# The reads of the preceding group ahead of the products of the group, in a vision tower with linear attention on one core

## The reference

```python
h = _L0_tok_ref(x, gamma, beta, W, b)                       # (64, 169, 128)
h = concatenate([cls_tok, h], axis=1)
# attention over layernorm(h): q, k, v = x Wq^T, x Wk^T, x Wv^T
def step(S, qkv):
    qt, kt, vt = qkv
    S = S + LR * einsum('bd,be->de', vt, kt)                # summed over the 64 images
    return S, einsum('de,be->bd', S, qt)
h = h + outs
h = h + ffn(layernorm(h))
```

## Time and profile before

| | us |
|---|---|
| median of 3 runs | 224.33 |
| lowest, highest | 224.09, 224.41 |
| span of the profiled execution | 221.7 |
| TensorE multiply busy | 198.4 (89%) |
| TensorE weight load busy | 168.0 (76%) |
| VectorE busy | 152.6 (69%) |
| GpSimd busy | 152.1 (69%) |
| ScalarE busy | 128.6 (58%) |

### The profile page before, as it was taken

How to read it: one execution, slowest core, us unless ns; L and a number is a source line. 1 busy time by engine, 2 the same in 40 slices (tenths; PEclk the granted TensorE clock), 3 DMA queues, 4 the chain that set the end, 5 groups by cost and what they waited for, 6 DMA issues and landing times.

```text
span 221.7 us, 5075 instructions
## 1 busy us (share of the span) xinstructions
PE 198.4 (89%) x1566; PEld 168.0 (76%) x1566; DVE 152.6 (69%) x760; ACT 128.6 (58%) x314; POOL 152.1 (69%) x125
## 2 busy tenths in 40 slices
PE   0699998999899999999999999999999999988700
PEld 0499897787688889888888888889888888876500
DVE  4549894453397694678687587669579578779681
ACT  4232637797533464475756575574665566467972
POOL 1029938796972899969999859949999253262641
PEclk9999999999999999999999999999999999999975
DMA  5999991924022004253052422012202202202156
GB/s 137 398 419 423 416 418 69 269 98 162 10 74 90 6 0 166 50 159 97 3 178 76 162 50 49 19 33 50 47 3 49 47 3 49 47 4 47 31 116 148
DMA packets 17074, 25.90 MB, mean 117 GB/s; under 512 B 1576, under 2 KB 13551, under 8 KB 16920
## 3 DMA queue, kind: packets, MB, share of 16 engines
q1 hardware_dynamic: 16300, 25.06, 35.0%
q10 hardware_dynamic: 748, 0.51, 0.8%
HBM read 19.65 MB, written 5.92 MB: 115 GB/s over the span
## 4 chain that ended last, share of the span: by engine, by line
PE 69%; DMA 9%; DVE 7%; ACT 5%; SPq 3%; issue 3%; POOL 1%; POOLq 1%; ACTq 0%; DVEq 0%
PE conv L542 31%; PE vr_ps L586 12%; PE outs L613 9%; DMA images<-x_rows 9%; PE first_ps L596 8%; PE turn L576 4%; DVE dve L1191 2%; PE conv L550 2%; ACT values L780 1%; ACT scaled L750 1%; PE conv L586 1%; SPq L461 1%; DVE state L951 1%; ACT g_t L744 1%; DVE state L943 1%
## 5 line engine op out<-in xcount | busy, mean ns | idle before, releaser
L542 PE MATMUL conv<-scaled,wt 128*128 128x256 f32 (+3 forms) x432 | 111.3, 373 | 7.4 <-DMA wt<-weight 7.2
L444 POOL TENSOR_TENSOR scaled<-rows,gam 128x832 f32<-128x832 f32 (+1 forms) x54 | 83.9, 1573 | 17.7 <-DMA rows<-x_windows 17.5
L542 PEld LDWEIGHTS conv<-scaled,wt 128*128 128x128 f32 x432 | 71.8, 193 | 15.8 <-DMA wt<-weight 7.2
L780 ACT ACTIVATE values<-vr_ps,rstd 128x256 f32<-128x256 f32 x76 | 36.0, 474 | 61.4 <-PE vr_ps L586 52.2
L1266 POOL TENSOR_TENSOR rstd<-var,powers 128x8 f32<-128x8 f32 (+2 forms) x20 | 30.3, 1516 | 27.2 <-DVE var L963 27.1
L943 DVE TENSOR_TENSOR state<-first_ps,state 128x128 f32<-128x128 f32 x80 | 23.3, 291 | 31.2 <-PE first_ps L596 26.4
L788 ACT ACTIVATE images<-images,ln_shift,ln_gain 128x128 f32<-128x128 f32 x82 | 38.0, 488 | 1.6 <-DVE ln_shift L1014 1.6
L1256 POOL TENSOR_TENSOR g_low<-g_t,g_high 128x512 fp32r<-128x512 f32 x21 | 26.7, 1271 | 8.2 <-ACT g_high L767 8.2
L586 PE MATMUL vr_ps<-w_high,g_low 128*128 128x256 f32 x78 | 31.1, 398 | 0.3 <-ACT values L780 0.3
L932 DVE BATCH_NORM_STATS2 ln_stats<-images 128x6 f32<-128x128 f32 x85 | 23.8, 285 | 6.7 <-ACT images L774 6.6
L951 DVE TENSOR_TENSOR state<-second_ps,state 128x128 f32<-128x128 f32 x80 | 22.6, 282 | 2.1
(11 more groups left out here) (175 smaller groups left out, 267.1 us busy)
## 6 DMA issues: line engine op xcount, KB each, us to landing
rows<-x_windows SPq DMA_DIRECT2D x12, 864.0 KB, 5.0
out<-images SPq DMA_DIRECT2D x40, 128.0 KB, 2.4
images<-x_rows SPq DMA_DIRECT2D x4, 832.0 KB, 14.7
images<-x_rows SPq DMA_DIRECT2D x1, 1040.0 KB, 14.2
images<-x_rows SPq DMA_DIRECT2D x1, 624.0 KB, 20.5
rows<-x_windows SPq DMA_DIRECT2D x1, 448.0 KB, 6.3
gam<-gamma SPq DMA_DIRECT2D x1, 422.5 KB, 7.0
bet<-beta SPq DMA_DIRECT2D x1, 422.5 KB, 7.5
```

Source lines behind the costliest of these rows:

```text
L444: return eng.tensor_tensor(scaled[:, s, at + skip:at + N], window[:, skip:N], gains.unsqueeze(2).to_broadcast([P, N - skip, B]), ALU.mult)
L542: last = pe.matmul(conv_ps[g % 2][:, at:at + n * B], held, scaled[:, s, a % RING:a % RING + n], start=first, stop=(g < EARLY and s >= TOP ...
L780: act.activation(values[:, t % VALUE_SLOTS].rearrange("p a e -> p (a e)"), vr_bank(t)[:, 0:2 * E], ACT.Identity, scale=rho_of(t)).then_inc ...
```

## The change

In the first step of a period the call of the reads of group g - 1, with its wait for h2_ready, now stands ahead of the products of group g. The wait for the states of the preceding group stays first. It holds for g = 1 to 17; g = 0 has no reads, and the tail is as it was. The unused name WARM goes, so that all line numbers behind it are lower by one.

```diff
--- before.py
+++ after.py
@@ -31,7 +31,6 @@
 
 EARLY = 5
 
-WARM = 14
 LEAD = 2
@@ -632,10 +631,10 @@
                 if i == 0 and g >= 0:
                     if g > 0:
                         pe.wait_ge(state_ready, states_to(t - 1))
-                    products(g)
                     if g > 0:
                         pe.wait_ge(h2_ready, tile_no(t - PER_GROUP - 1))
                         reads(g - 1)
+                    products(g)
```

## The result

| | kernel before | changed kernel |
|---|---|---|
| median of 9 runs, us | 224.09 | 225.47 |
| span of the profiled execution, us | 221.7 | 223.4 |

The ratio of changed to before is 1.0079 with a 95% interval of 1.0051 to 1.0107: 0.8% slower, some 1.8 us by the ratio, 1.4 us by the medians and 1.6 us by the two spans before rounding (the last store is issued at 218.16 us in the kernel before and at 219.76 us in the changed one). The forecast was 1.49 us more and 225.8 us. In several kernels a few runs lie 1.7 to 2.7 us above the median; the ratios count them as well, and their intervals are the wider for it.

The account below looks back on a forecast made before the run. The prediction took TensorE to bound the kernel, with 198.4 us of work in a 221.7 us span. To the median of 224.33 us it added 0.46 and 1.03 us, giving 225.8 us, range 224.5 to 227.0.

Parts of the forecast that it names:

- TensorE's own time: Swapped blocks on TensorE keep their lengths behind new neighbours: 0 us, bounded at about 0.1 us in a period.
- What comes earlier: Reads end 1.09 us sooner, but add_out on VectorE stands behind later state sums, so nothing gains: 0 us.
- The first loss: At g = 1, VectorE's sum of group 4 ends later, so TensorE's turn of that group loses 0.46 us.
- The second loss: GpSimd's gapless string from g = 2 delays the power for group 6 and TensorE's vr product at g = 5: 1.03 us.
- The 0.32 us of waiting: TensorE's vr product at 94.93 us already waits 0.32 us in the kernel before, so that place has no room.
- Where it just fits: Other places, such as reads waiting for add_out, later vr products, scales and the tail, have just enough room: 0 us.
- the fit that was told as 0.00: After GpSimd's next long string, TensorE's vr product at 127.15 us is possible exactly when due: room 0.00, no loss.
- The sum: Whole kernel: 0.46 and 1.03 us added, span 223.2 us, median 225.8 us, 0.66% slower.
- B: GpSimd's string starts from something else or TensorE catches up: 0.46 us or less, 224.3 to 224.8 us; chance 0.11.
- C: TensorE's new block joins hide exposed weight loads: 0.1 us gained per period and join, down to 223.4 us; chance 0.06.
- D: Tight fits tip over or a TensorE join costs 0.1 us more: 226.1 to 227.0 us; chance 0.13.
- E: The new TensorE stop at 95 us, about 1.3 us long, drops its clock to 1.2 GHz: near 229 us; chance 0.02.

Follow-up runs that it names:

- only1: Kernel before with reads moved ahead of products at g = 1 alone; +0.46 us between two fixed TensorE rows, ratio 1.0043 to the kernel before.
- only2: Kernel before with reads moved ahead of products at g = 2 alone; +1.01 us between two fixed TensorE rows, ratio 1.0028 to the kernel before.
- after_pool: Changed kernel with four GpSimd scales moved behind the powers for groups 5 and 6; +0.20 us between two fixed TensorE rows, ratio 1.0009 to kernel before.
- not12: Kernel before with reads moved ahead of products only at g = 3 to 17; 0.00 us between two fixed TensorE rows, ratio 1.0006 to kernel before.
- after_both: Changed kernel with whole(g) ahead of VectorE's moments and four GpSimd scales behind the powers; median 223.06 us, ratio 0.9944 to the kernel before.
- before_both: Kernel before with whole(g) ahead of VectorE's moments and four GpSimd scales behind the powers; median 223.01 us, ratio 0.9947 to the kernel before.

## Why the prediction was right

**TensorE's own time, 0.** Right: 1.03 and 1.09 us in the new order, and 0.02 us between the two orders when both places have room. The bound of 0.1 us in a period was far wider than needed.

**What comes earlier, 0.** Right: the reads of group 5 start at 102.31, add_out of its group on VectorE follows its state sums as before, and net of the start-up no instruction of VectorE, ScalarE or GpSimd behind the turn of group 0 starts earlier than before by more than 0.02 us.

**The first loss, 0.46 us.** Right: 0.46 us in only1 and between the rows at 66 us.

**The second loss, 1.03 us more.** Right in its sum and its place, with 1.01 us in only2. The 0.32 us of waiting that it read at this place before were there, but were worth 0.26 us (after_pool). The prediction told one step less than there is: the loss comes in two parts. The first vr behind the power for group 5 loses 0.3 us (below, 0.81 us behind the convolution where before it was 0.52), and the one behind the power for group 6 the rest. Both hang on the same string, and what the first takes the second no longer has to.

```profile
86.68 0.82 PE L541 MATMUL conv<-scaled,wt 128*128 128x128 f32 x4
87.49 0.36 PE L585 MATMUL vr_ps<-w_high,g_low 128*128 128x256 f32 x1
```

**Where it just fits, 0.** Right on the whole. The vr product behind the fit that was told as 0.00 starts here:

```profile
128.73 0.47 PE L585 MATMUL vr_ps<-w_high,g_low 128*128 128x256 f32 x1
```

That is 1.58 us behind the 127.15 of the earlier trace rows, and the vr product before it, 125.19 against 123.62, was 1.57 us late already: the fit held. From 96.48 to the tail the delay grows from 1.55 to 1.60 us in steps of 0.01 or 0.02 us, too small to name a cause.

**The sum.** 1.49 us forecast, 1.53 us by the ruler, 1.6 us by the spans, of which 0.07 us is the start-up. The 225.8 us lie 0.3 us above the median of the runs, mainly because the median of before was 224.33 us in the three runs that the forecast started from, and 224.09 in nine.

**The rivals.** B (no change) fell with only1 and only2, C and D (the joins) with the block lengths and not12, and E with the first row of the clock below: TensorE is busy 1.75 of 2.5 us around the new stop, and the granted clock stays at its full level, 2.4 GHz. The row that the prediction leaned on had only 0.66 us without work, half of the stop of 1.3 us that it foresaw, so it couldn't speak against E by itself. Measured, the new stop is 1.45 - 0.35 = 1.10 us from start to start, 0.75 us of it idle. The rule of the Trainium skill that the prediction weighed here ("TensorE: Matmul & The Clock Gate", section "What's actually happening": idleness lowers the clock) isn't contradicted by it: this stop did not set it off, but with no TensorE work at all from 216 to 220 us the granted clock is at its lower level, 1.2 GHz (the second row).

```profile
94.50:97.00 2.50, 1.75 (x18) 1.26 (x15) 0.48 (x4) 1.14 (x3) 2.50 (x2) 1.00 0.00 0
...
216.00:220.00 4.00, 0.00 (x0) 0.00 (x0) 2.16 (x15) 3.06 (x8) 1.60 (x2) 0.50 0.47 108
```

## What to carry to other kernels

To move a block ahead of another on a saturated engine cost that engine nothing by itself here, and delayed by the block's length all that hangs on the other one. Follow that chain to each of its dates with the saturated engine, and look above all for an engine that works through a gapless string: it hands a delay at its head on in full, here from one period to an event three periods later, past any room that the periods between seem to have. If such a date has no room, the cure is in the helpers' orders (what is due first goes first), which here took 1.25 us off the kernel before and 2.76 us off the changed one.

## What was not expected of the hardware

The first 41 us of an execution, with the large loads, scatter by up to 0.8 us (the turn of group 0 at 41.01 to 41.80 us over kernels that are the same up to there, but for VectorE's and GpSimd's order in some, and over more than one chip), while in the 162 us behind them two pairs of kernels that should agree (before and not12, after_both and before_both) differ by 0.00 and 0.02 us. By these executions two spans of one execution each can't be compared below 0.8 us, while distances between two rows of the same instructions behind the first 41 us can, to some 0.05 us.
